# A two-layer language-model tower on one core: token units with EW half 0 in the scores' bank, a new order on ScalarE and VectorE, and decode blocks at other FFN tiles

## What is computed

```
enc = one_hot(x, 512) + pe
for l in range(4):
    q, k = enc @ Wq[l], enc @ Wk[l]
    sims = where(causal, q @ k.T / sqrt(128), -1e9)
    enc = softmax(sims) @ enc
```

## Time and profile before

| | us |
|---|---|
| median of 3 runs (lowest, highest) | 2463.64 (2461.04, 2465.51) |
| profiled execution | 2462.3 |
| its span, first to last instruction | 2460.3 |
| TensorE busy | 2323.6 |
| VectorE busy | 1654.4 |
| ScalarE busy | 788.6 |
| GpSimd busy | 376.2 |

### The profile page before, as it was taken

How to read it: one execution, slowest core, us unless ns; L and a number is a source line. 1 busy time by engine, 2 the same in 40 slices (tenths; PEclk the granted TensorE clock), 3 DMA queues, 4 the chain that set the end, 5 groups by cost and what they waited for, 6 DMA issues and landing times.

```text
span 2460.3 us, 32611 instructions
## 1 busy us (share of the span) xinstructions
PE 2323.6 (94%) x12610; PEld 1202.9 (49%) x12610; DVE 1654.4 (67%) x3165; ACT 788.6 (32%) x1683; POOL 376.2 (15%) x416
## 2 busy tenths in 40 slices
PE   5877799999999999889999999999999997999999
PEld 3666444444444444434455555555555554444444
DVE  6577599998999787676465555555555565778623
ACT  5576412122121113333343333333333332211111
POOL 2353100000000412630040004002100300411000
PEclk9898899999999999999999999999999998999999
DMA  4554623333332440200020001001100100100001
GB/s 161 171 172 171 227 92 114 125 121 114 122 120 86 163 165 33 78 31 19 27 69 1 1 1 69 1 2 35 35 1 1 52 1 1 56 1 1 1 1 69
DMA packets 50799, 166.71 MB, mean 68 GB/s; under 512 B 4048, under 2 KB 16976, under 8 KB 41680
## 3 DMA queue, kind: packets, MB, share of 16 engines
q1 hardware_dynamic: 50640, 164.56, 18.9%
HBM read 137.28 MB, written 27.26 MB: 67 GB/s over the span
## 4 chain that ended last, share of the span: by engine, by line
PE 80%; DVE 12%; ACT 4%; issue 2%; POOL 1%; DMA 1%; SPq 0%; DVEq 0%; ACTq 0%
PE ps L678 19%; PE ps L239 13%; PE ps L1289 7%; PE ps L690 7%; PE ps L1114 6%; PE ps L1101 6%; PE ps L571 4%; PE ps L929 3%; PE ps L946 3%; PE ps L1135 2%; PE ps L253 2%; PE ps L408 2%; PE ps L261 2%; PE ps L251 1%; PE ps L536 1%
## 5 line engine op out<-in xcount | busy, mean ns | idle before, releaser
L678 PE MATMUL ps<-planes 128*128 128x512 f16 x1224 | 270.0, 379 | 1.4 <-DVE work L735 1.4
L678 PE MATMUL ps<-planes,wa 128*128 128x512 f16 x1080 | 239.2, 380 | 5.2 <-DMA wa<-rw 5.2
L239 PE MATMUL ps<-planes,wa 128*128 128x512 f16 x840 | 201.5, 385 | 5.1 <-DVE planes L1576 5.1
L678 PEld LDWEIGHTS ps<-planes 128*128 128x128 f16 x1224 | 119.5, 98 | 143.4 <-DVE work L735 2.3
L239 PE MATMUL ps<-planes 128*128 128x512 f16 x768 | 180.9, 379 | 1.5 <-issue 1.5
L718 ACT ACTIVATE work<-work 128x512 f16<-128x512 f32 x64 | 40.3, 630 | 442.2 <-DVE work L751 442.2
L678 PEld LDWEIGHTS ps<-planes,wa 128*128 128x128 f16 x1080 | 106.0, 98 | 131.6 <-issue 7.5
L516 POOL TENSOR_TENSOR rstd<-rstd,half 128x4 f32<-128x4 f32 x16 | 17.1, 1071 | 871.1 <-DVE rstd L511 871.1
L294 ACT ACTIVATE ps<-ps,nmax 128x128 f32<-128x128 f32 x160 | 54.5, 341 | 295.4 <-DVE nmax L288 295.3
L833 DVE COPY_PREDICATED work<-work 128x1024 f32<-128x1024 int16 x144 | 120.4, 836 | 21.6 <-DVE work L833 0.8
L946 PE MATMUL ps<-wa,work 128*128 128x512 f16 x512 | 124.6, 387 | 9.0 <-DVE h L976 9.0
(11 more groups left out here) (193 smaller groups left out, 4442.3 us busy)
## 6 DMA issues: line engine op xcount, KB each, us to landing
planes<-rw SPq DMA_DIRECT2D x17, 2048.0 KB, 7.9
wa<-rw SPq DMA_DIRECT2D x15, 2048.0 KB, 7.3
stg<-in_rw_w SPq DMA_DIRECT2D x32, 512.0 KB, 3.8
stg<-in_ff_w SPq DMA_DIRECT2D x16, 1024.0 KB, 5.1
rw<-wa SPq DMA_DIRECT2D x16, 1024.0 KB, 7.0
stg<-in_mo_w SPq DMA_DIRECT2D x16, 1024.0 KB, 4.8
work<-in_glu_idx SPq DMA_DIRECT2D x48, 128.0 KB, 2.1
glu_dec<-work SPq DMA_DIRECT2D x48, 128.0 KB, 1.7
```

Source lines behind the costliest of these rows:

```text
L239: mm = te.matmul(ps[:, bank, :], w(i, kt), x(j, kt), start=(kt == 0 and n == 0), stop=(kt == KT - 1 and n == 2))
L678: mm = te.matmul(ps[:, what, :], rw_w(q, what, i, kt, m), mix[what][j][:, kt, at:at + CH], start=(kt == 0 and z == 0), stop=(kt == KT - 1 ...
```

## The change

- `tok_ew` half 0 goes to bank 2, the scores' bank, where the unit before is of layer 1 or more; it waits for `probs` of the unit instead of `pr_lo` of the one before, which half 1 now waits for. The scores (`tok_scores`) are made in bank 3 first, then, behind the low half of EW half 0, in bank 2. Output tiles move from banks 2 and 3 to 3 and 6.
- Unit 0: the projection of unit 1 stands ahead of the transposes. At `LN_UNIT` the scores stand ahead of the LN transposes.
- ScalarE: rows and the |w| sum stand behind q and k, the weight split between the transposed probabilities and EW half 1; the sum of unit 8 is in unit 4. VectorE: columns are made behind q and k and finished behind the maxima. The columns end in unit 3.
- The mixing of the first chunk is cut into single steps, strewn among units 13 to 15.
- The first two token weights are issued by ScalarE's queue, the rest of the token columns earlier by SyncE's; the first load of head weights one piece earlier.
- `FF_DEC`: the FFN's nine decode blocks stand at other tiles. On SyncE two loads of attention weights move ahead of the second block's store.

ScalarE, unit 1, before: q and k of unit 2, EW, probabilities, their transposes, EW, exponentials, columns, |w| sum, weight split.

```diff
+        def ew_bank(u, b):
+            return 7 if b == 1 else 6 if u == 0 or TOK[u - 1][0] == 0 else 2
+
         def tok_ew(pe, u, b):
...
             if b == 0:
                 pe.wait_ge(enc_lo, KT * (c + 1))
                 pe.wait_ge(w_ready, l + 2)
+                if ew_bank(u, 0) == 2:
+                    pe.wait_ge(probs, u + 1)
+            else:
                 if u > LN_UNIT:
                     pe.wait_ge(ln_done, TPC)
                 if u > 0 and nth(*TOK[u - 1], (1, 2)) > 0:
                     pe.wait_ge(pr_lo, nth(*TOK[u - 1], (1, 2)))
+                if u in OUT_AT:
+                    pe.wait_ge(to_free, TPC * OUT_AT.index(u) + 2)
             if k > 0:
                 pe.wait_ge(ew_lo, 2 * k - 1 + b)
-            if u in OUT_AT:
-                pe.wait_ge(to_free, TPC * OUT_AT.index(u) + b + 1)
...
-        TO_BANK = [(6, 7, 2, 3), (6, 7, 2, 3), (6, 7, 0, 1), (6, 7, 4, 5)]
+        TO_BANK = [(6, 7, 3, 6), (6, 7, 3, 6), (6, 7, 0, 1), (6, 7, 4, 5)]
...
-        FF_DEC = (3, 15, 17, 21, 31, 34, 38, 47, 50)
+        FF_DEC = (15, 23, 27, 31, 39, 43, 47, 55, 59)
...
+        def mix_lo_dve(dve, e):
+            dve.wait_ge(mix_hi, e + 1)
+            ve.tensor_tensor(mix_dst(e, 1), mix_out(e), mix_dst(e, 0), ALU.subtract).then_inc(mix_lo, 1)
+
+        def mix_hi_act(act, e):
+            act.wait_ge(mix_y, e + 1)
+            se.activation(mix_dst(e, 0), mix_out(e), ACT.Copy).then_inc(mix_hi, 1)
...
-        COLS_AT = {0: (8, 9), 1: (10, 11), 2: (12,), 3: (13, 14), 4: (15,)}
-        ABS_AT = (0, 1, 2, 3, 8, 10, 11, 13)
-        ROWS_AT = {4: (0, 1, 2), 5: (3, 4, 5), 6: (6, 7, 8), 7: (9, 10, 11), 8: (12, 13), 9: (14, 15)}
+        COLS_AT = {0: (8, 9), 1: (10, 11), 2: (12, 13), 3: (14, 15)}
+        ABS_AT = (0, 1, 2, 3, 4, 10, 11, 13)
+        ROWS_AT = {4: (0, 1, 2), 5: (3, 4, 5), 6: (6, 7, 8), 7: (9, 10, 11), 8: (12, 13, 14, 15)}
...
+        def tok_scores(pe, u, ew0):
+            pe.wait_ge(q_split, u + 1)
+            pe.wait_ge(k_split, u + 1)
+            for b in range(2):
+                t0 = b * S
+                for n, (i, j) in enumerate(PASSES):
+                    te.matmul(ps[:, 3, b * S:b * S + S], qs[i][:, t0 + P:t0 + S], ks[j][:, t0:t0 + S], start=(n == 0), stop=(n == 2))
+            if ew0:
+                pe.wait_ge(ew_lo, ew0)
...
         def tok_pe(pe):
...
+            tok_scores(pe, 0, 0)
+            tok_ew(pe, 0, 0)
+            tok_project(pe, 1)
+            pe_transpose_probs(pe, 0)
+            tok_ew(pe, 0, 1)
+            tok_scores(pe, 1, 0)
+            for u in range(1, MU - 2):
...
+                pe_transpose_probs(pe, u)
+                if u in OUT_AT:
+                    pe.wait_ge(to_free, outs_before(u + 1))
+                tok_scores(pe, u + 1, 2 * nth(l, c, (0, 1, 2)) - 1 if l < LAYERS - 1 and ew_bank(u, 0) == 2 else 0)
+                if l < LAYERS - 1:
+                    tok_ew(pe, u, 1)
                 if u == LN_UNIT:
                     pe.wait_ge(pr_lo, nth(*TOK[u - 1], (1, 2)))
                     pe.wait_ge(ew_lo, 2 * nth(*TOK[u - 1], (0, 1, 2)))
                     ln_chunk(pe, ln_pe, 0, 0)
-                if u in OUT_AT:
-                    pe.wait_ge(to_free, outs_before(u + 1))
-                pe_scores(pe, u + 1)
-                if l < LAYERS - 1:
-                    tok_ew(pe, u, 1)
...
         def tok_act(act):
...
-                if u == MU - 3:
-                    mix_act(act, 0, 1)
-                    mix_act(act, 0, 2)
-                    rw_split_act(act, u)
-                if u >= 4 and u in ABS_AT:
+                rows_act(act, ROWS_AT.get(u - 1, ()))
+                if u in ABS_AT:
                     tok_act_abs(act, ABS_AT.index(u))
...
+                tok_act_pT(act, u)
                 if u == LN_UNIT:
                     ln_chunk(act, mix_act_copy, 0, 0)
+                else:
+                    rw_split_act(act, u)
...
+            for e in range(7, 12):
+                mix_hi_act(act, e)
             rw_split_act(act, u)
             tok_act_out(act, 3)
...
-            sp.dma_start(stg[:, 0, 0:1024], a["tok_w"][0]).then_inc(stg_full[0], 16)
-            sp.dma_start(stg[:, 1, 0:1024], a["tok_w"][1]).then_inc(stg_full[1], 16)
+            sp.dma_start(tok_cols[:, CH:NTOK], a["tok_cols"][:, CH:NTOK]).then_inc(cols_in, 16)
...
+            for j in range(RW_PIECES - 1):
+                if j == RW_PIECES - 2:
+                    load_rw(0)
...
-            store_dec(i + 1)
             for k in range(2):
                 sp.wait_ge(w_ready, WR_MO + k - 1)
                 sp.dma_start(stg[:, k, :], a["mo_w"][k]).then_inc(stg_full[k], 16)
+            store_dec(i + 1)
             store_dec(i + 2)
...
         @block.scalar
         def _(act):
+            se.dma_start(stg[:, 0, 0:1024], a["tok_w"][0]).then_inc(stg_full[0], 16)
+            se.dma_start(stg[:, 1, 0:1024], a["tok_w"][1]).then_inc(stg_full[1], 16)
             tok_act(act)
```

More of the change, by code:

```diff
@@ L461, in tok_out @@
                     pe.wait_ge(probs, u + 1)
+                if c < 2 and n == 3:
+                    pe.wait_ge(to_free, TPC * c + 1)
                 if c == 3 and n < 2:
@@ L1628, in tok_dve @@
+            dve_q(dve, 1)
+            dve_k(dve, 1)
+            cols_dve(dve, COLS_AT[0])
+            tok_dve_ew(dve, 0, 1)
+            dve_max(dve, 1)
+            cols_lo(dve, COLS_AT[0])
+            dve_norm(dve, 1)
+            for u in range(1, MU - 2):
+                l, c = TOK[u]
                 dve_q(dve, u + 1)
                 dve_k(dve, u + 1)
-                if u == MU - 3:
-                    mix_dve(dve, 0, 1)
-                    mix_dve(dve, 0, 2)
-                if 0 < u and l < LAYERS - 1:
+                cols_dve(dve, COLS_AT.get(u, ()))
+                if l < LAYERS - 1:
@@ L1857, in _ @@
             for u in range(MU):
-                for r in ROWS_AT.get(u, ()):
+                for r in ROWS_AT.get(u - 1, ()):
                     pool.wait_ge(row_hi, r + 1)
```

245 lines of the change are left out of this document (141 added, 104 removed).

## The result

| | before | changed |
|---|---|---|
| median of 5 runs (lowest, highest), us | 2463.44 (2461.04, 2465.51) | 2450.79 (2450.03, 2454.47) |
| ratio to before, 95% interval | | 0.9950 (0.9937 to 0.9963) |
| profiled execution, us | 2462.3 | 2450.03 |
| TensorE busy, us | 2323.6 | 2312.6 |

The changed kernel is 12.6 us faster. The prediction had 20.6 us (2443 from 2463.6), range 2427 to 2459.

A forecast was written before the change was run, and what follows sets the result against it. TensorE was taken to bound nearly all, with idle time only in token units and FFN. Term 1 to Term 4 gave 24.8 us, cut to 22; Term 5 lost 1.4: 2441.7 profiled, 2443 us median, range 2427 to 2459.

The forecast's parts named there:

- Term 1: Start to unit 3's projection: weights arrive sooner, but the second |w| sum waits for its load; 2.8 us lost.
- Term 2: Units 3 to 9: EW half 0 in bank 2 shortens the cycle from 13.9 to about 12.1 us; 18.5 gained.
- the lock: Token units: port pair shared by VectorE and GpSimd, which stretch each other; 3 us taken off the gain.
- Term 3: Units 10 to 12: unit 13's scores, now ahead of the LN transposes, wait some 6 us; 4.6 us lost.
- Term 4: Units 13 to first head: waits of 4.72, 6.20, 5.17 us go, 2.3 and 2.7 come; 13.7 us gained.
- Term 5: FFN: 21.1 us gained at old waits, against the late eighth load's 18.4 to 20.1 wait; 1.4 lost in all.
- if additions still stop TensorE: FFN: sign that the prediction is wrong; it expected no TensorE waits at residual additions, 9.0 us before.
- (a): Token units: ScalarE bounds them, so Term 2 and Term 4 give half; 16 us less, 2458; chance 0.15.
- (b): FFN: the wait for the eighth load doesn't come; 21 us more gained, 2422; chance 0.09.
- (c): FFN waits return at 15 us, the new wait stays, token gain 20 us less: 2478; chance 0.08.
- (d): Token units: waits yield fully without clock loss, 33 us in place of 22, 2432; chance 0.68 together with the forecast.

The follow-up runs named there:

- `combined_b2`: Changed kernel with five of the edits together, plus the first |w| sum moved out of unit 0 and splits one unit later; 2440.04 us, ratio 0.9901.

## Why the prediction was right, and where it was off

The direction and the range held: 2450.8 lies in 2427 to 2459. The size was off: 12.6 us, not 20.6. The place of the gain held too: with the old FFN blocks the token stage keeps its gain, and with the new blocks alone nothing is gained. Of the five terms, 3 and 5 came out at their size partly by luck, as said below.

- **Term 1** (start to unit 3, -2.8): -1.2. The mechanism held: the projection starts at 61.71 (forecast 63.3, before 60.48), ScalarE waits 1.95 us for the second sum's load, and with the sum away the projection starts 10 us sooner. The start is 10.92, near the forecast 10. But of the 2.3 us against 13.19 in the kernel before, the queue accounts for 1.2; the order of the columns differs too, and what it is worth by itself wasn't tried. Two traces with the old start begin at 13.19 and 12.91, so the start itself scatters by 0.3 us.
- **Term 2** (units 3 to 9, +18.5) is the term that was mis-sized: 11.0. The step that failed is the one that put the split in front of EW half 1 at no cost. I took VectorE's durations from the kernel before, where GpSimd ran beside other work. With the splits at the unit's end, the cycle is 12.07 us and the stretch from unit 3's projection to the first output product takes 106.7 us instead of 110.6. That is 3.9 of the missing 7.5 (kernels with the changed token code scatter from 110.0 to 113.2 there). The rest lies in waits, five of 1.3 to 2.1 us in that run, and their clock, and wasn't taken apart. I had named the lock and taken off 3 us for all of it. What the gain itself owes to bank 2 wasn't tried by itself either: the waits for the low half in banks 6 and 7 (2.84, 2.19 and 2.21 us before, at 81.87, 129.09 and 157.99) are gone in the changed kernel, but no run takes back the bank alone.
- **Term 3** (-4.6): -4.4, right by its size and not by its place, which is luck. The 6 us that I put at the scores of unit 13 came as 6.40 at unit 11's row product, from a queue that I hadn't followed: GpSimd behind a LayerNorm step, the load behind GpSimd, the split behind the load. Without it, my wait appears, at half its size: 3.12 us (6.10 where a split stretches the normalised tiles). The stretch then takes 42.28 us, against 43.61 before and the 48.2 that the prediction gave it.
- **Term 4** (+13.7): 10.4. The three old waits are gone. The new one is 3.06 us at unit 14's transposes (forecast 2.3). The 2.7 us that I forecast as new for the last unit is 1.96, and it stood there before as well, as did 2.10 us at the last output product, with 18 slow matmuls behind it (5.73 us now):

```profile
266.41 0.87 PE L261 MATMUL ps<-ident,work 128*128 128x128 f32 x6 [1.91 <-DVE work L307]
...
272.77 5.72 PE L468 MATMUL ps<-planes 128*128 128x512 f16 x18 [2.10 <-DVE planes L1612]
```

So these two are no cost of the change. Where the other 3.3 us went stays open. What I missed is behind the first head's start: 1.6 us given back, at the wait for the first decode block and in the slow matmuls behind it.

- **Term 5** (-1.4): -1.5. The wait for the eighth load is 18.41 us, within 18.4 to 20.1, for the reason given, and mending SyncE's order gave 19.5 us. With that wait away the FFN stretch gains 18.7 us against the kernel before, where the prediction comes to 19.6 (21.1 less 1.5). It is a sum of misses that cancel, in part by luck: the wait of 3.99 us goes whole where I counted 2.1, and one at an addition stays. Of the three residual additions one still stops TensorE, for 5.40 us: "if additions still stop TensorE" is met there, by a block stretched from 6.6 to 15 us. I had put 1.5 us for blocks beside GpSimd's splits; moving that block gave 6.3 us in the FFN.
- **Rivals.** (a), ScalarE bounds the token stage, had 2458 (2459, with the 16 us that it names); 2450.8 is midway between it and the forecast. Its mechanism was only half there: where ScalarE was late it mostly stood waiting for a load (3.92 and 1.95 us for the first two sums, 6.38 and 3.22 at unit 11), and it was busy 171 of 267.82 us. (b) and (c) fall: the wait came, and two of the three additions' waits went. (d), no clock loss, falls too.

## What to carry over

When work moves between places, move its loads on the issuing queue as well: twice here (the eighth weight load, the sums of `combined_b2`) a store or a wait for the moved step held back an unrelated load, for 19.5 and for 27 us. A step that can wait for a transfer doesn't belong ahead of a copy that the bounding engine needs, even if its own duration looks free. And where two engines slow each other, as VectorE and GpSimd do here, durations belong to a place in the order and not to an instruction: look up beside what it will run.

## What the runs showed of the hardware that was not expected

- VectorE's subtractions and sums slow beside GpSimd by operand: 1086 against 745 ns and 1511 against 690 with both inputs in SBUF, 683 in either case with one in PSUM. But two inputs aren't needed: decode picks (7.03 against 2.67 us) and three normalised tiles (4.03 against 1.45) read a single large operand from SBUF and slow more. No view here shows in which mode these ran.
- The same FFN code took 281.8 or 287.3 us; at least the 3.1 us of it in one wait go with when GpSimd's splits met the decode block of tile 21. Effects of edits were therefore not additive: the new block places gained nothing in the old kernel (0.9996), while going back to the old ones in the changed kernel was no gain either, though it took away a wait of 18 us.
- Behind waits of 5.65, 6.76 and 6.12 us the same 24 matmuls of 512 columns took 6.98, 7.56 and 8.14 us in three kernels that are alike there, and the marks some 35 us on lay up to 3.3 us apart.
